# Reordering the weight and look-up stage of a pairwise-interaction recommender kernel

## What is computed

```python
x1 = einsum('bik,bjk,hij->bhk', e,  e, W1) + b1      # W1: 128 x 26 x 26
x2 = einsum('bik,bjk,hij->bhk', x1, e, W2) + b2      # W2: 128 x 128 x 26
z  = sum over k of concat(x1, x2)                    # 256 numbers a sample
h  = relu(concat(z, dense_ctx) @ W_top1 + b_top1)    # 272 -> 512
h  = relu(h @ W_top2 + b_top2)                       # 512 -> 256
y  = h @ W_top3                                      # 256 -> 1
```

## Time and profile before

| | us |
|---|---|
| median of 3 runs (lowest to highest) | 255.42 (255.09 to 255.67) |
| the profiled execution's own time | 255.76 |
| its span (first to last instruction) | 253.8 |
| TensorE busy | 147.2 |
| VectorE busy | 107.4 |
| ScalarE busy | 88.3 |
| GpSimd busy | 85.4 |

### The profile page before, as it was taken

The page is one execution under the profiler, slowest core; times in us unless marked ns, Lnnn a source line. Parts: engine busy times, 40 slices in busy tenths (PEclk is TensorE's granted clock), DMA queues, the critical chain, the costliest instruction groups (busy, mean ns, idle before and its releaser), DMA issues.

```text
span 253.8 us, 3289 instructions
## 1 busy us (share of the span) xinstructions
PE 147.2 (58%) x1169; PEld 129.5 (51%) x1169; DVE 107.4 (42%) x397; ACT 88.3 (35%) x295; POOL 85.4 (34%) x96
## 2 busy tenths in 40 slices
PE   0784001300003243020058999999999999999995
PEld 0772001000001131000034899998999899989994
DVE  6940019100000003000049998992589458945401
ACT  2540001000010401040037779857447744774112
POOL 3877777777777777771000000000000000000000
PEclk9999555555555586555558999999999999999999
DMA  6650000000010100000000020100000000000000
GB/s 193 230 109 13 13 14 14 13 13 13 13 13 14 18 13 13 13 13 5 0 0 0 0 87 0 21 0 4 0 15 7 3 0 15 6 0 3 12 9 2
DMA packets 7350, 5.86 MB, mean 23 GB/s; under 512 B 3473, under 2 KB 6805, under 8 KB 7206
## 3 DMA queue, kind: packets, MB, share of 16 engines
q1 hardware_dynamic: 4230, 3.86, 5.1%
q0 software_dynamic: 2816, 1.45, 3.9%
q10 hardware_dynamic: 288, 0.35, 0.5%
HBM read 5.18 MB, written 0.00 MB: 20 GB/s over the span
## 4 chain that ended last, share of the span: by engine, by line
PE 46%; another core or an unknown queue 29%; issue 12%; ACT 8%; DMA 3%; SPq 0%; ACTq 0%
PE p_zh L888 12%; PE p_t L868 12%; PE p_t L876 7%; DMA region<-in_L_rec_W 3%; ACT e_diag L325 3%; PE p_x L930 3%; PE p_t L843 2%; PE p_zh L843 2%; PE p_zh L896 2%; PE p_t L828 1%; ACT region L416 1%; PE p_x L888 1%; PE p_x L941 1%; PE p_t L960 1%
## 5 line engine op out<-in xcount | busy, mean ns | idle before, releaser
L303 POOL DMA_INDIRECT rows<-in_tbl,idx x88 | 84.5, 960 | 29.3 <-issue 26.5
L843 PE MATMUL p_zh<-S,region 128*128 128x352 f32 (+1 forms) x26 | 13.2, 641 | 54.6 <-issue 29.5
L843 PE MATMUL p_t<-S,region 128*128 128x352 f32 (+1 forms) x26 | 14.4, 682 | 40.9 <-ACT region L416 22.3
L630 DVE TENSOR_TENSOR region<-region 128x14 f32<-128x14 f32 (+10 forms) x11 | 2.9, 303 | 81.0 <-issue 51.1
L843 PEld LDWEIGHTS p_zh<-S,region 128*128 128x128 f32 x26 | 6.2, 257 | 60.7 <-issue 60.1
L843 PEld LDWEIGHTS p_t<-S,region 128*128 128x128 f32 x26 | 6.2, 262 | 47.5 <-issue 46.8
L888 PE MATMUL p_zh<-region 124*128 124x128 f32 x256 | 29.6, 277 | 0.0
L888 PEld LDWEIGHTS p_zh<-region 124*128 124x128 f32 x256 | 28.9, 192 | 0.5
L325 ACT COPY e_diag<-eT 32x160 f32<-32x160 f32 (+2 forms) x80 | 28.6, 358 | 0.8
L333 ACT COPY region<-p_t 124x352 f32<-124x352 f32 x32 | 14.5, 452 | 20.6 <-PE p_t L868 19.8
L760 DVE COPY L<-p_t 74x208 f32<-74x208 f32 x24 | 8.9, 371 | 22.8 <-PE p_t L876 22.8
(11 more groups left out here) (118 smaller groups left out, 249.8 us busy)
## 6 DMA issues: line engine op xcount, KB each, us to landing
region<-in_L_rec_W SPq DMA_DIRECT2D x1, 1664.0 KB
rows<-in_tbl,idx POOLq DMA_INDIRECT x88
wt<-in_W_top SPq DMA_DIRECT2D x1, 512.0 KB
region<-in_W_top SPq DMA_DIRECT2D x1, 512.0 KB
region<-in_tbl SPq DMA_DIRECT2D x4, 125.0 KB
w<-in_L_rec_W ACTq DMA_DIRECT2D x1, 338.0 KB, 3.3
gmix<-L SPq DMA_DIRECT2D x4, 56.0 KB
gmix<-L SPq DMA_DIRECT2D x4, 30.0 KB
```

Source lines behind the costliest of these rows:

```text
L303: pool.indirect_dma_start(rows[:, t, f * EMB:(f + 1) * EMB], None, tables[f], bass.IndirectOffsetOnAxis(ap=idx[:, t, f:f + 1], axis=0),).t ...
L843: last = nc.tensor.matmul(p_f[n % 2][:, j1 - 1 - j, 0:width], w2T[:, j, :], S[:, 0:width], start=True, stop=True)
```

## The change

Nothing of what is computed changes. The ids of tile 0 are loaded alone, on SP's queue; those of the other tiles go first on ScalarE's queue, ahead of W1, and GpSimd waits for them before tile 1. GpSimd also makes a column of zeros, from which ScalarE clears the first `e_diag`; VectorE clears the second at its very start. The sum of W1 is done in two halves, before the ids are split, and the small copies that end S stand after the one-hot columns of tile 0. On TensorE slice 0 of F comes straight after the transposes of W2, and the four look-ups stand after slices 0, 4, 7 and 11. VectorE spreads groups 3 and 4 of tile 0 itself; `choose(1)`, `choose(2)`, the ones of the second diagonal and the first two turns of rows of tile 1 are put among its sums, `choose(3)` behind its saves of WT. Banks of PSUM are reassigned accordingly, and the waits ahead of `dense_part` are moved into `z_sums`.

```diff
+        zero = sb("zero", [P, 1])
...
-        p_wt = [p_t[0][0], p_w, p_x, p_t[1][0]]
-        p_over, p_rows = p_t[1] + [p_z2, p_h1], [p_x, p_w, p_x, p_h1]
...
+        p_wt = [p_t[0][0], p_w, p_t[1][0], p_t[0][1]]
+        p_over, p_rows = p_t[1] + [p_z2, p_h1], [p_x, p_w, p_w, p_x]
...
-            sp.dma_start(idx[:, :, :], ids.rearrange("(p t) f -> p t f", t=TILES)).then_inc(ids_in, 16)
+            sp.dma_start(idx[:, 0, :], ids.rearrange("(p t) f -> p t f", t=TILES)[:, 0, :]).then_inc(ids_in, 16)
...
+            nc.gpsimd.memset(zero[:, :], 0.0).then_inc(zero_made, 1)
...
             for t in range(TILES):
+                if t == 1:
+                    pool.wait_ge(ids_rest_in, 16)
                 for g in range(NG):
                     for f in gathered(g):
...
+            act.dma_start(idx[:, 1:TILES, :], ids.rearrange("(p t) f -> p t f", t=TILES)[:, 1:TILES, :]).then_inc(ids_rest_in, 16)
             act.dma_start(w1[:, :, :], W1).then_inc(w1_in, 16)
             act.dma_start(S[:, 0:1], b1.unsqueeze(1), allow_slow_non_contiguous=True).then_inc(b1_in, 16)
+
+            act.wait_ge(zero_made, 1)
+            nc.scalar.copy(e_diag[0].rearrange("p s q c -> p (s q c)"),
+                           zero[:, :].to_broadcast([P, STEPS * QUADS * COLS])).then_inc(diag_zero[0], 1)
...
-                if n == 0:
+                if n == 1:
                     save_dense()
-                if n == 1:
...
-                if n == 4:
+                if n == 5:
                     spread(0, 1)
                 if n == 9:
                     spread(0, 2)
-                if n == 13:
-                    spread(0, 3)
-            spread(0, 4)
...
-            diag_zeros(0)
-            diag_ones(0)
+            nc.vector.memset(e_diag[1][:, :, :, :], 0.0).then_inc(diag_zero[1], 1)
...
                 dve.wait_ge(ids_in, 16)
+                dve.wait_ge(ids_rest_in, 16)
...
-                nc.vector.tensor_tensor(pair_sum[:, :, :], w1[:, :, :], w1[:, :, :].rearrange("p l m -> p m l"), ALU.add
-                                        ).then_inc(s_sum, 1)
-                dve.wait_ge(s_sum, 1)
+                nc.vector.tensor_tensor(pair_sum[:, l0:l1, :], w1[:, l0:l1, :],
+                                        w1[:, :, l0:l1].rearrange("p l m -> p m l"), ALU.add).then_inc(s_sum, 1)
+
+            def first_diagonal():
...
+                dve.wait_ge(s_sum, 2)
                 nc.vector.tensor_copy(pair_sum[:, :, :].rearrange("p l m -> p (l m)")[:, ::FIELDS + 1],
                                       w1[:, :, :].rearrange("p l m -> p (l m)")[:, ::FIELDS + 1]).then_inc(s_diag, 1)
...
+            first_sums(0, FIELDS // 2)
+            dve.wait_ge(ident_ready, 1)
+            nc.vector.tensor_copy(ident_b[:, :], ident[:, :]).then_inc(ident_b_ready, 1)
+            dve.wait_ge(count_made, 2)
+            nc.vector.tensor_copy(count[:, :], count_i[:, :]).then_inc(count_ready, 1)
+            first_sums(FIELDS // 2, FIELDS)
+            first_diagonal()
             split_rows()
-            first_sums()
-            for t in range(TILES):
+            for q in range(QUADS):
+                diag_ones(0, q)
+            one_hot(0)
+            first_weights()
+            for t in range(1, TILES):
                 one_hot(t)
-            first_weights()
...
+            def spread(t, g):
+
+                f0, f1 = GROUPS[g]
+                for q in range(QUADS):
+                    part = slice(q * EMB, (q + 1) * EMB)
+                    last = nc.vector.tensor_copy(e_diag[t % 2][part, :, q, slot(f0):slot(f1)], eT[part, :, f0:f1])
+                last.then_inc(diag_ready, 1)
...
+            choose(1)
             group(0, 2)
             for m in reversed(range(A, 20)):
                 high_pairs(m)
-            diag_zeros(1)
             group(0, 3)
+            spread(0, 3)
             group(0, 4)
-            choose(1)
+            spread(0, 4)
+
             top_fields()
+            diag_ones(1, 0)
             top_pairs()
             middle_first()
+            choose(2)
...
             middle_second()
+            diag_ones(1, 1)
             low_pairs_first(4, CUT)
+            rows_to_columns(1, 0)
             low_pairs_first(0, 4).then_inc(low_first, 1)
             dve.wait_ge(low_first, 1)
-            low_pairs_second()
+            low_pairs_second(1, 6)
+            diag_ones(1, 2)
+            low_pairs_second(6, CUT)
+            diag_ones(1, 3)
             own_high_rows(0, CUT)
+            rows_to_columns(1, 1)
             low_of_middle_pairs()
             middle_low("low").then_inc(wsym_ready, 1)
             dve.wait_ge(wsym_ready, 1)
             pairs_static(1)
-            diag_ones(1)
-            choose(2)
-            choose(3)
             dve.wait_ge(small_in, 16 * SMALL)
             nc.vector.tensor_scalar(bias_k[:, :], bias[:, 0:2], float(EMB), None, ALU.mult).then_inc(bias_ready, 1)
...
+            for i in range(1, WT_BANKS, 2):
+                dve.wait_ge(wt_done, i + 1)
+                nc.vector.tensor_copy(WT[0:ROWS0, 4 * i:4 * i + 4, :],
+                                      p_wt[i % 4][0:ROWS0, :].rearrange("p (s h) -> p s h", h=P)).then_inc(wt_saved[1], 1)
+            choose(3)
             for t in range(1, TILES):
-                rows_to_columns(t, 0)
-                rows_to_columns(t, 1)
-                if t == 1:
-
-                    for i in range(1, WT_BANKS, 2):
-                        dve.wait_ge(wt_done, i + 1)
-                        nc.vector.tensor_copy(WT[0:ROWS0, 4 * i:4 * i + 4, :],
-                                              p_wt[i % 4][0:ROWS0, :].rearrange("p (s h) -> p s h", h=P)
-                                              ).then_inc(wt_saved[1], 1)
+                if t > 1:
+                    rows_to_columns(t, 0)
+                    rows_to_columns(t, 1)
                 rows_to_columns(t, 2)
...
-            pe.wait_ge(w2t_saved, 4)
-            pe.wait_ge(table_in, 16 * NL)
-            look_up(0)
-            pe.wait_ge(hot_ready, 2 * TILES)
             pe.wait_ge(s_ready, 1)
...
-                if n >= 2:
+
+                if n < 2:
+                    pe.wait_ge(hot_ready, 4 * (n + 1))
+                else:
                     pe.wait_ge(f_saved, n - 1)
...
                 if n == 0:
+                    pe.wait_ge(w2t_saved, len(W2T))
+                    pe.wait_ge(table_in, 16 * NL)
+                    look_up(0)
+                if n == 1:
                     pe.wait_ge(dense_in, 16)
-                    pe.wait_ge(w2t_saved, 5)
                     for t in range(TILES):
                         last = nc.tensor.matmul(p_t[0][0][0:DENSE, t * P:(t + 1) * P], dense_rows[:, t, :], ident[:, :],
                                                 start=True, stop=True)
                     last.then_inc(dense_t, 1)
                 if n == 4:
-                    pe.wait_ge(w2t_saved, len(W2T))
                     look_up(1)
-            pe.wait_ge(chosen_ready, 1)
-            look_up(2)
-            pe.wait_ge(f_saved, len(SLICES) - 1)
-            look_up(3)
+                if n == 7:
+                    pe.wait_ge(chosen_ready, 2)
+                    look_up(2)
+                if n == 11:
+                    look_up(3)
 
...
+                for s in range(SLOTS):
+                    if t == 0 and s % 4 == 0:
+                        pe.wait_ge(wt_saved[s // 4 % 2], s // 8 + 1)
+                    if s != Z1_ONE:
+                        last = nc.tensor.matmul(p_z2[:, 0:P], WT[0:ROWS0, s, :], T[0:ROWS0, t % 2, s, :],
+                                                start=False, stop=(s == SLOTS - 1), skip_group_check=True)
+                last.then_inc(z2_done, 1)
+                if t == 0:
+                    pe.wait_ge(rows_ready, TILES)
                 pe.wait_ge(mix_in[t], 16 * MOVES)
...
+                if i == 3:
+                    pe.wait_ge(t_saved[0], TURNS)
...
-            pe.wait_ge(rows_ready, TILES)
             pe.wait_ge(top_in, 16 * 4)
             dense_part(0)
-            pe.wait_ge(wt_saved[0], -(-WT_BANKS // 2))
-            pe.wait_ge(wt_saved[1], WT_BANKS // 2)
```

More of the change, by code:

```diff
@@ L317, in spread @@
                     if t < 2:
-                        act.wait_ge(static_ready[t], 2)
+                        act.wait_ge(static_ready[t], 1 + QUADS)
                     else:
@@ L474, in _, with diag_ones @@
         def _(dve):
-            def diag_zeros(n):
-                nc.vector.memset(e_diag[n][:, :, :, :], 0.0).then_inc(diag_zero[n], 1)
-            def diag_ones(n):
+            def diag_ones(n, q):
                 dve.wait_ge(diag_zero[n], 1)
-                for q in range(QUADS):
-                    last = nc.vector.memset(e_diag[n][q * EMB:(q + 1) * EMB, :, q, 0:COLS:COLS - 1], 1.0)
-                last.then_inc(static_ready[n], 1)
+                nc.vector.memset(e_diag[n][q * EMB:(q + 1) * EMB, :, q, 0:COLS:COLS - 1], 1.0).then_inc(static_ready[n], 1)
```

(21 more changed lines are left out.)

8 lines of the change are left out of this document (4 added, 4 removed).

## The result

The changed kernel takes **260.26 us** (260.19 to 260.55, 4 runs) against 255.43 beside it: ratio 1.0192, 95% interval 1.0175 to 1.021. It is slower by 4.8 us where 254.2 was forecast. The profiled execution has a span of 258.3 us, 4.5 longer than before.

What follows compares the result with a forecast made beforehand. It took late release of TensorE's products during the gathers, then TensorE itself from 128.84, as the bound. From 255.76 profiled, -1.3 and +0.1 gave 254.56, or 254.2 us against the median; forecast case 253.4 to 255.2, stated range 252.6 to 256.9.

Steps and rivals of the forecast that it cites:

- Ids of tile 0 alone: Start of GpSimd's gathers: a quarter of the ids, issued before W1, lands sooner; -1.0 us, at best 1.85 gained.
- W1's sum halves: VectorE beside the third gather: two sums of 0.73 us slow the gathers less than one of 1.45; -0.3 us.
- Window's end follows the gathers: The stretch when TensorE's products are released some 20 us late ends 1.3 us earlier, as the gathers do; chance 0.44.
- 13 us on top: Time between the last gather's end at 115.47 and the end of late release at 128.8.
- first rival: Late release still ends at 128.8 despite earlier gathers, leaving only +0.1: 255.5 us; chance 0.23.
- Order inside the window: TensorE during late release: same products reordered, 20 from 16.3 on, slice 4 released before the end; 0 us.
- second rival: Slice 4 is released too late, so slice 7 starts 1.3 us later: 256.8, or 255.5 with an earlier end; chance 0.20.
- 5.6 us for each product: Release rate during late release, from 13 products between 37.11 and 109.81 (72.70 us).
- tight, but in time: Verdict that 20 products from 16.3 on take 112 us, to 128.3, just before late release ends.
- F behind the window: TensorE after late release: look-ups inside F fill two waits but no longer cover slice 14's save; +0.1 us.
- VectorE's list in time: VectorE after late release finishes its longer list at 156.4, before TensorE wants `wsym` at 157.5; 0 us.
- Large gain: Rival: slices ahead of the opening look-up are released promptly, dropping 21.8 us of waiting: 232 us; chance 0.09.

Runs made afterwards that it cites:

- a_fixed: Changed kernel with VectorE's old order and the other tiles' ids on SyncE's queue between tile 0's and W2: 254.98 us against 259.95, ratio 0.9807.
- a_w1_first_3: Changed kernel with W1 first on ScalarE's queue, ids of tiles 1 to 3 behind it and b1: 261.01 us against 259.95 before, one run.
- b_no_tile3_2: Kernel before without tile 3's 22 gathers (tile 3 reads tile 2's rows): 227.09 us against 259.95, one run.
- a_again: Changed kernel, unchanged, run once more with a profile: 260.49 us against 255.93 for the kernel before, ratio 1.0177.
- b_f_first_2: Kernel before with all gathers behind F and ScalarE's five tile 0 spreads after its F saves: 268.41 us against 259.95, one run.
- b_pause: Kernel before with gathers paused after tile 0's until F is saved, ScalarE's five tile 0 spreads following: 255.93 us against 261.31, ratio 0.9791.

## Why the prediction was wrong, point by point

- **Ids of tile 0 alone, -1.0.** Measured -1.39 at the first gather (3.06 for 4.45). But that gain is the other side of W1's delay: with W1 first again the first gather starts at 4.26 (a_fixed) and 4.40 (a_w1_first_3). This is the step that failed first. It priced what standing ahead of W1 gives to the ids and put at nothing what it takes from W1: landing in 7.7 us instead of 3.3, and its sum now stands in VectorE's queue ahead of everything that TensorE starts with. TensorE's first products started at 11.54 instead of 6.96.
- **W1's sum halves, -0.3.** Measured -1.2: no gather of 2.17 us is left. Together the gathers end 2.6 us earlier instead of 1.3.
- **Window's end follows the gathers.** Right, and shown by b_no_tile3_2. The "13 us on top" were two things: 7 to 11 us from the last gather's start, then a backlog. My first rival (end unmoved) is out. It leaned on the Trainium skill, "SBUF — State Buffer", section "Who interferes with whom", which says that TensorE never waits on anyone. Here its results came out at 2.80 us a record while gathers ran. Whether SBUF has any part in that, and so whether the rule itself is broken, no run shows.
- **Order inside the window, 0.** This is where the loss arises: the list of products began with slice 0, since the transposes were taken to be through by 16. Measured, the last of them was saved at 86.16 and slice 0 at 91.77; most cost 2.8 us each, and slices 1 to 4, look-up 1 and the end of look-up 0 fell behind the window. The term was put at 0 and measured +7.0. The second rival named this kind of loss, one slice for 1.3 us; it was four slices and more. The count also took 5.6 us for each product of look-up 0, though its eight were released by 37.11 in the kernel before, so in 2.7 each at most; the prediction's "tight, but in time" rested on a price that was too high there and on a list that was too short. Why the transposes were caught stays open, as said above.
- **F behind the window, +0.1.** The step itself held: the wait for slice 14's save is 0.90, slice 7 waits 0.61. But the piece was no longer the same.
- **VectorE's list in time.** Held in relation to the turns, though all of it came some 4 to 5 us later than forecast: `wsym` was ready at 161.3, TensorE transposes it at 161.75, right behind its turns. Tile 1's last product ended at 178.23 and its first turn began at 178.92: 0.7 of room, 0.6 forecast.
- **Large gain.** It came nowhere.

## What to carry over

Before moving a load ahead of another, ask what the other one now lands behind, and who is queued in front of an in-order engine that waits for it: here 39 KB put ahead of W1 held back all of TensorE's start by 4.6 us. Where a stretch has a price per instruction, count all kinds of instructions that can slip into it, in the units that the profile counts, not only those that stand there now. And run the kernel before again beside every experiment: the same kernel took 153 and 261 us here, and a ratio against another day's time would have made any theory true.

## What the runs showed of the hardware

- In some groups of runs TensorE's results were released at 2.80 us a record while GpSimd's indirect gathers ran, the same for a transpose (128 columns), half an fp32 product of 352 or 415 columns and the turns (108 and 72 columns). In other groups, one of them on the same chip, the same gathers held nothing back.
- Neither level of the granted clock explains it: in the kernel before the clock was granted in full from 15.3 to 25.5 us, while slice 0, issued at 18.22, was released at 42.61; and between half rate and full the same four records take 2.69 and 1.35 us, where here they took 11.2.
- The onset is gradual: four transposes took 5.6, 7.1, 8.4, then 11.2 us in a_again and 4.3, 7.0, 8.4, 10.5, then 11.2 in a_w1_first_3. It follows the gathers' start by no fixed time (prompt at 72.83 in b_f_first_2, 34 us into the gathers; late from 77.4 in b_pause, 20 us into them). What sets it, and which state of a chip it needs, is open.
- Beside the 1664 KB of W2, what is issued first lands early and what comes second on ScalarE's queue pays: 338 KB of W1 took 3.1 to 3.8 us when first and 7.7 to 8.2 when issued 0.4 us later behind 39 KB of ids; these took 1.8 to 2.0 us when first and 8.2 behind W1 and b1.
